# Self-attention's folded values as three fp32r passes over 128 tokens, with odd heads in swapped sequence order

## The reference, cut to what matters

```python
qkv = x @ w_qkv                      # 16 heads of 64, x is the layernormed residual
scores = einsum('bhid,bhjd->bhij', q, k) / sqrt(64)
attn = softmax(where(mask, scores, -inf), axis=-1)   # mask is causal for 64 tokens
out = einsum('bhij,bhjd->bhid', attn, v)
x = x + out.reshape(b, s, 1024) @ w_out
```

## Time and profile before

| | |
|---|---|
| median of 3 runs | 2475.48 us (2474.33 to 2478.04) |
| the profiled execution | 2475.1 us |
| its span, first to last instruction | 2473.1 us |
| PE busy | 2310.8 us, 93% of the span |
| DVE busy | 2117.5 us, 86% |
| mean granted TensorE clock | 0.974 |

### The profile page before, as it was taken

One profiled execution on the slowest core, in us unless ns is written; L12 is line 12 of the kernel. 1 busy time (PEld: TensorE's weight loads), 2 busy tenths in 40 slices (PEclk: granted clock), 3 DMA queues, 4 the chain that ended last, 5 costly groups with the idle time before them and its releaser, 6 DMA issues. The chain is left out here.

```text
span 2473.1 us, 57460 instructions
## 1 busy us (share of the span) xinstructions
PE 2310.8 (93%) x16359; PEld 1935.2 (78%) x16359; DVE 2117.5 (86%) x3384; ACT 1333.1 (54%) x2566; POOL 1528.0 (62%) x1117
## 2 busy tenths in 40 slices
PE   6988999999999999999999999999999998999842
PEld 3666888888888888888888888888888878776522
DVE  6779999998999999999999999999999995576657
ACT  4744555555555555555555555555555534355440
POOL 3424777777777777777777777777777750011155
PEclk8999999999999999999999999999999999999965
DMA  2432122222222222222222222222222226220000
GB/s 81 164 121 47 43 52 58 55 53 53 53 53 52 53 61 53 52 52 52 61 53 53 56 63 52 53 53 52 52 52 52 52 80 191 70 70 2 2 1 17
DMA packets 441099, 145.04 MB, mean 59 GB/s; under 512 B 365344, under 2 KB 423616, under 8 KB 440896
## 3 DMA queue, kind: packets, MB, share of 16 engines
q1 hardware_dynamic: 440880, 143.50, 23.4%
q10 hardware_dynamic: 144, 0.52, 0.1%
HBM read 109.17 MB, written 34.73 MB: 58 GB/s over the span
## 5 line engine op out<-in xcount | busy, mean ns | idle before, releaser
L451 POOL TENSOR_TENSOR probs<-arena,best_all 128x1024 f32 (+2 forms) x397 | 944.0, 2378 | 420.8 <-DVE best L817 398.9
L1061 PEld LDWEIGHTS u_ps<-rows,probs 128*128 128x128 f32 x6656 | 800.1, 191 | 54.7 <-issue 13.3
L1061 PE MATMUL u_ps<-rows,probs 128*128 (+1 forms) x6656 | 810.8, 275 | 9.1 <-ACT probs L648 5.0
L802 DVE SCALAR_TENSOR_TENSOR arena<-s_ps,mask,rrms 128x512 f32 (+2 forms) x832 | 604.0, 727 | 113.4 <-PE s_ps L938 111.7
L648 ACT ACTIVATE probs<-probs 128x1024 f32<-128x1024 f32 (+1 forms) x416 | 441.0, 1061 | 415.0 <-POOL probs L451 401.7
L778 DVE TENSOR_REDUCE ssq<-squares 128x16 f32<-128x1024 f32 (+1 forms) x416 | 501.2, 1205 | 34.7 <-ACT squares L606 34.7
L606 ACT ACTIVATE squares<-k_ps 128x512 f32<-128x512 f32 (+1 forms) x832 | 451.3, 591 | 50.1 <-DVE ssq L778 25.1
L817 DVE TENSOR_TENSOR best<-best,arena 128x1024 f32<-128x1024 f32 (+1 forms) x352 | 446.3, 1268 | 0.1
L936 PE MATMUL k_ps<-w_hi,cT_hi 128*128 128x512 f32 (+1 forms) x832 | 361.9, 435 | 12.4 <-ACT squares L606 12.3
L487 POOL TENSOR_TENSOR cT_lo<-cT,cT_hi 128x128 fp32r<-128x128 f32 (+1 forms) x416 | 296.9, 714 | 107.3 <-ACT cT_hi L600 107.3
L936 PE MATMUL s_ps<-q_hi,cT_hi 128*128 (+2 forms) x832 | 330.4, 397 | 2.1 <-DVE arena L802 1.8
(11 more groups left out here) (224 smaller groups left out, 2174.4 us busy)
## 6 DMA issues: line engine op xcount, KB each, us to landing
stage<-in_ctx SPq DMA_DIRECT2D x1536, 16.0 KB, 1.7
rows<-in_ctx SPq DMA_DIRECT2D x32, 768.0 KB
queries<-probs SPq DMA_DIRECT2D x16, 1024.0 KB, 4.0
q_plain<-queries SPq DMA_DIRECT2D x32, 512.0 KB, 3.3
best_all<-best_rows SPq DMA_DIRECT2D x31, 512.0 KB, 3.6
u_transposed<-uT_sb SPq DMA_DIRECT2D x124, 128.0 KB, 2.6
a_uT<-u_transposed SPq DMA_DIRECT2D x10, 1024.0 KB, 4.9
arena<-u_transposed SPq DMA_DIRECT2D x6, 1024.0 KB, 5.0
```

The costliest lines, as they stand in the source:

```text
L451: pool.tensor_tensor(probs[0:r, slot_of(c, PRING), :], scores_at(b, c), best_all[0:r, bass.ds((b % 2) * HL, HL)], ALU.subtract).then_inc(s ...
L802: dve.scalar_tensor_tensor(out=scores_at(p, c, h * HALF, HALF).rearrange("p (h l) -> p h l", l=L), in0=s_ps[h][0:r, :].rearrange("p (h l) ...
L1061: last = pe.matmul(u_ps[g // 3][:, at:at + UW], probs[0:r, s, g * P:(g + 1) * P], rows, start=(c == 0 and g % 3 == 0), stop=(c == NC - 1), ...
```

## The change

The folded values are computed in the same way as q and k: both operands are split into an fp32r high part and a low part, and each bank gets three fp32r matmuls of all 128 tokens by 512 columns. With 128 tokens as the stationary operand, the sequence b lands on PSUM partitions 64b to 64b+63. `mix` needs even and odd heads on different rows, so for the odd heads the tokens are taken in swapped order. To have the swapped order as one slice, each tile now takes 192 columns of yT_hi and yT_lo: its 128 tokens and its first 64 again. Which head of a pair a row group r serves is now `r ^ b` in `score` and `mix`; the probability tiles, the banks a_sc and a_ov and v2 are laid out by r instead of by odd.

- Gone: the tile yT and its copy on ACT (L1296, 128x128), the semaphore yT_ready.
- New on ACT: a copy of 128x64 for each tile, and in steps -9 to -6 one copy of 128x512 (wvo2_hi).
- New on DVE: a subtraction of 128x64 for each tile, and in steps -9 to -6 one subtraction of 128x512 (wvo2_lo), ahead of the quantizing.
- PE: `project_v` issues 12 fp32r matmuls of 128x128 by 128x512 instead of 8 fp32 ones of 128x64 by 128x512; `project_qk` reads its 512 tokens as four pieces of 128 with a step of 192; the order of array rows in `score` changes for b = 1.

```diff
@@ self_attention, PE
             def project_v(t, i):
-                pe.wait_ge(yT_ready, t + 1)
+                pe.wait_ge(yT_lo_ready, 2 * t + 2)
+                pe.wait_ge(wvo2_ready, 4)
...
-                    b, h = divmod(k, 2)
-                    at = t % 12 * P + b * L
-                    for odd in range(2):
-                        last = pe.matmul(four[k][odd * L:(odd + 1) * L, :], yT[:, at:at + L],
-                                         w["wvo2"][:, odd * HL + h * HALF:odd * HL + (h + 1) * HALF], start=True, stop=True)
-                    last.then_inc(v_ps, 1)
+                    tokens = window(t, k // 2)
+                    pe.matmul(four[k][:, :], yT_hi[:, tokens], wvo2_hi[:, half(k)], start=True, stop=False)
+                    pe.matmul(four[k][:, :], yT_lo[:, tokens], wvo2_hi[:, half(k)], start=False, stop=False)
+                    pe.matmul(four[k][:, :], yT_hi[:, tokens], wvo2_lo[:, half(k)], start=False, stop=True).then_inc(v_ps, 1)
@@ score
-                        for odd in range(2):
+                        for r in range(2):
+                            odd = r ^ b
                             rows = slice(odd * HD, (odd + 1) * HD)
-                            last = pe.matmul(sc[odd][b * L:(b + 1) * L, g * L:(g + 1) * L], q[rows, g, mine], k[rows, g, mine],
+                            last = pe.matmul(sc[r][b * L:(b + 1) * L, g * L:(g + 1) * L], q[rows, g, mine], k[rows, g, mine],
@@ mix
-                        for odd in range(2):
-                            rows = slice(odd * L, (odd + 1) * L)
+                        for r in range(2):
+                            rows = slice(r * L, (r + 1) * L)
...
-                            last = pe.matmul(ov[odd][b * L:(b + 1) * L, 0:D], w["pT"][rows, at:at + L],
-                                             w["v2"][t % 2][rows, b * HL + g * D:b * HL + (g + 1) * D],
+                            odd = r ^ b
+                            last = pe.matmul(ov[r][b * L:(b + 1) * L, 0:D], w["pT"][rows, at:at + L],
+                                             w["v2"][t % 2][rows, odd * HL + g * D:odd * HL + (g + 1) * D],
@@ ACT, step i
-                    act.activation(yT_hi[:, at:at + P], work[1][:, 0:P], ACT.Copy).then_inc(yT_hi_ready, 1)
...
-                    act.activation(yT[:, at:at + P], work[1][:, 0:P], ACT.Copy).then_inc(yT_ready, 1)
+                    act.activation(yT_hi[:, window(t)], work[1][:, 0:P], ACT.Copy).then_inc(yT_hi_ready, 1)
+                    act.activation(yT_hi[:, again(t)], work[1][:, 0:L], ACT.Copy).then_inc(yT_hi_ready, 1)
+                if -9 <= i < -5:
+                    part = half(i + 9)
+                    act.activation(wvo2_hi[:, part], w["wvo2"][:, part], ACT.Copy).then_inc(wvo2_hi_ready, 1)
@@ DVE, step i
-                    dve.wait_ge(yT_ready, t + 1)
...
-                    dve.tensor_tensor(yT_lo[:, at:at + P], work[1][:, 0:P], yT_hi[:, at:at + P], ALU.subtract).then_inc(yT_lo_ready, 1)
+                    dve.wait_ge(yT_hi_ready, 2 * t + 2)
+                    dve.tensor_tensor(yT_lo[:, window(t)], work[1][:, 0:P], yT_hi[:, window(t)], ALU.subtract).then_inc(yT_lo_ready, 1)
+                    dve.tensor_tensor(yT_lo[:, again(t)], work[1][:, 0:L], yT_hi[:, again(t)], ALU.subtract).then_inc(yT_lo_ready, 1)
...
+                if -9 <= i < -5:
+                    part = half(i + 9)
+                    dve.wait_ge(wvo2_hi_ready, i + 10)
+                    dve.tensor_tensor(wvo2_lo[:, part], w["wvo2"][:, part], wvo2_hi[:, part],
+                                      ALU.subtract).then_inc(wvo2_ready, 1)
```

More of the change, by code:

```diff
@@ L1154 @@
 QK_PARTS = 4
+WINDOW = P + L
 def upto(step, ahead, most=TILES):
@@ L1185, in self_attention @@
         wqk_lo = sb("a_wqk_lo", [P, 2 * HL], F32R)
-        yT_hi = sb("a_yT_hi", [P, 2 * HALF], F32R)
-        yT_lo = sb("a_yT_lo", [P, 2 * HALF], F32R)
-        yT = sb("a_yT", [P, 3 * HALF])
+        yT_hi = sb("a_yT_hi", [P, 2 * 4 * WINDOW], F32R)
+        yT_lo = sb("a_yT_lo", [P, 2 * 4 * WINDOW], F32R)
+        wvo2_hi = sb("a_wvo2_hi", [P, 2 * HL], F32R)
+        wvo2_lo = sb("a_wvo2_lo", [P, 2 * HL], F32R)
         uT = sb("a_uT", [P, 2, 2 * HL])
@@ L1210, in self_attention @@
         y_var, y_log, y_rough, y_ready, y_turned = (sem(f"a_{n}") for n in ("y_var", "y_log", "y_rough", "y_ready", "y_turned"))
-        yT_hi_ready, yT_ready, yT_lo_ready = sem("a_yT_hi_ready"), sem("a_yT_ready"), sem("a_yT_lo_ready")
+        yT_hi_ready, yT_lo_ready = sem("a_yT_hi_ready"), sem("a_yT_lo_ready")
+        wvo2_hi_ready, wvo2_ready = sem("a_wvo2_hi_ready"), sem("a_wvo2_ready")
         qk_ps, qk_saved, v_ps, v_saved = sem("a_qk_ps"), sem("a_qk_saved"), sem("a_v_ps"), sem("a_v_saved")
@@ L1227, in p_of, with window, again, group @@
             return w["p"] if t % 2 == 0 else p_odd
+        def window(t, swapped=0):
+            at = t % 8 * WINDOW + swapped * L
+            return slice(at, at + P)
+        def again(t):
+            at = t % 8 * WINDOW + P
+            return slice(at, at + L)
+        def group(part, j):
+            at = j % 2 * 4 * WINDOW
+            return part[:, at:at + 4 * WINDOW].rearrange("p (t n) -> p t n", n=WINDOW)[:, :, 0:P]
         def by_head(ap):
@@ L1334, in softmax_shift @@
             def softmax_shift(t):
-                p3 = p_of(t)[:, :].rearrange("p (h q j) -> p h q j", q=2, j=L)
+                p3 = p_of(t)[:, :].rearrange("p (h r j) -> p h r j", r=2, j=L)
                 if t >= 2:
@@ L1448, in turn_y @@
                 pe.wait_ge(qk_saved, parts_upto(i - 1))
-                pe.wait_ge(yT_lo_ready, t)
+                pe.wait_ge(yT_lo_ready, 2 * t)
                 pe.transpose(work[1][:, 0:P], y[:, t % 3 * D:(t % 3 + 1) * D], ident[:, :]).then_inc(y_turned, 1)
             def project_qk(j, r, i):
-                pe.wait_ge(yT_lo_ready, 4 * j + 4)
+                pe.wait_ge(yT_lo_ready, 2 * (4 * j + 4))
                 pe.wait_ge(w_ready, 1)
@@ L1461, in project_qk @@
                     if k == 3:
-                        pe.wait_ge(yT_lo_ready, upto(i, TURN_Y_AHEAD))
+                        pe.wait_ge(yT_lo_ready, 2 * upto(i, TURN_Y_AHEAD))
                     g = slice((4 * r + k) * P, (4 * r + k + 1) * P)
[L1464 to L1467, removed]
+                    pe.matmul(four[k][:, :], wqk_hi[:, g], group(yT_hi, j), start=True, stop=False)
+                    pe.matmul(four[k][:, :], wqk_hi[:, g], group(yT_lo, j), start=False, stop=False)
+                    pe.matmul(four[k][:, :], wqk_lo[:, g], group(yT_hi, j), start=False, stop=True).then_inc(qk_ps, 1)
             def project_v(t, i):
-                pe.wait_ge(yT_ready, t + 1)
+                pe.wait_ge(yT_lo_ready, 2 * t + 2)
+                pe.wait_ge(wvo2_ready, 4)
                 for k in range(4):
@@ L1487, in score @@
                 pe.wait_ge(qk_saved, 16 * (t // 4) + 16)
-                for odd in range(2):
-                    pe.wait_ge(masked, max(0, 2 * (t - 1) + odd + 1))
+                for r in range(2):
+                    pe.wait_ge(masked, max(0, 2 * (t - 1) + r + 1))
                 q, k = (w["qk"][j][:, n * 4 * HL:(n + 1) * 4 * HL].rearrange("p (g n) -> p g n", n=HALF) for n in range(2))
```

9 lines of the change are left out of this document (3 added, 6 removed).

## The result

The change makes the kernel faster, by a quarter of a percent: the median is 2468.55 us (2464.43 to 2473.08, 9 runs), that of the kernel before in the same rounds 2474.33 (2469.16 to 2478.04, 9 runs), a ratio of 0.9975 [0.9964, 0.9986]. The profiled execution took 2468.55 too, with a span of 2466.8. The forecast was 2470.0, its range 2467.6 to 2476.0. Of all executions behind this document one, in e7, was in a slow state and took 4671.11 us; its ratio leaves it out.

The account below looks back on a forecast made before the run. PE was taken to set the pace where folded values are computed, with ACT's last save 0.34 us ahead of it. Terms 1.64-1.44-1.20-1.32-2.58-0.64 = -5.54 took 2475.1 to 2469.6; with 0.4 for the median, 2470.0 us, range 2467.6 to 2476.0.

Parts of the forecast that it names:

- The folded values: PE from the folded values' start to the scores: 3.58 us becomes 2.84, saving PE 0.83 a tile.
- The start: Steps -9 to -5: DVE's new subtractions are on the path in steps -7 and -6, costing +1.64 us, bounds 1.1 and 2.1.
- The third 0.14: Part of the start's cost: the second yT_lo in step -5, ahead of PE's fourth qk bank, costs 0.14 us.
- Steps -4 to -1: Steps -2 and -1 gain 0.83 us each, less 0.08 and 0.14 for the longer yT_lo: -1.44.
- Steps 0 to 5: ACT's v saves hold the period at 14.06 us, PE idles 0.63; 0.20 gained per step, -1.20 in all.
- Step 6 and steps 7 to 10: Step 6 gains 1.32 us through an earlier mask and cheaper folded values; steps 7 to 10, with alternating periods, gain 2.58.
- The tail: Steps 11 on: only step 12, 9.27 us from `turn_p` to the mask, gains, 0.64; the others none.
- Rival 1: Score block doubles from 1.09 to 2.18 us as both row groups write each bank: 2481.3 us, 8%; small stretch 13%.
- Rival 2: Longer PE idle before `sum_heads` in step -5 brings half clock onto the path: cost 1.5 to 2.8 us, 12%.
- Rival 3: Nothing waits for ACT, so PE gains 0.83 us in all 13 steps from -2 to 10: 2465.9 us, 6%.
- Rival 4: The second yT_lo runs after POOL's pass, so steps 0 to 5 gain nothing: 2471.2 us, 7%.

Follow-up runs that it names:

- e7: Changed kernel without the values' middle pass (yT_lo times wvo2_hi), `turn_p` waiting only for the first two v banks: 2452.62 us, ratio 0.9924 to the kernel before.
- e10: Changed kernel with one plain fp32 matmul of 128 tokens per v bank, the tokens' low part left out: 2472.14 us, ratio 0.9996 to the kernel before.
- e8: Changed kernel with only DVE's wvo2_lo subtractions moved to steps -9, -8, -4 and -3, ACT's copies unmoved: 2465.35 us, ratio 0.9965 to the kernel before.
- e4: Changed kernel with DVE's wvo2_lo subtractions and ACT's wvo2_hi copies in steps -9, -8, -4 and -3: 2466.8 us, ratio 0.9979 to the kernel before.
- e1: Changed kernel with `turn_p` waiting only for the first two v banks to be saved: 2465.48 us, ratio 0.9969 to the kernel before.
- e6: Changed kernel without the middle pass of the folded values (yT_lo times wvo2_hi), wait of `turn_p` kept: 2461.54 us, ratio 0.996 to the kernel before.
- e2: Kernel before the change, with `turn_p` waiting only for the first two v banks to be saved: 2472.93 us, ratio 1.0006 to the kernel before.
- e11_after_again: Changed kernel timed again unaltered, as baseline of the third set: 2466.55 us, ratio 0.9974 to the kernel before.
- e3: Kernel before the change, folded values still plain fp32, with only the new row order in `score` and `mix`: 2472.2 us, ratio 1.0 to the kernel before.
- e5: Changed kernel with both the shorter `turn_p` wait of e1 and the later wvo2 split of e4: 2462.87 us, ratio 0.9964 to the kernel before.
- e9: Changed kernel with DVE's later subtractions of e8 and the shorter `turn_p` wait of e1: 2462.04 us, ratio 0.9955 to the kernel before.

## Why the prediction was right, point by point

- **The folded values.** Forecast 2.84, measured 2.81. e10 shows that the old block's price was that of plain fp32 and not of the pairs: 0.88 a bank is 3.8 passes of 0.229, so the saving is about one pass in four. The Trainium skill, "FP8 and Floating Point Precision", section "TensorE Precision Notes", gives true FP32 four passes through the array; the 3.8 of e10 agrees.
- **The start.** +1.64 was +1.30. Right in kind: each of the two steps grew, e8 takes the two subtractions away from there and gets 1.20 back. The pitch of wvo2_lo was 0.60, the second yT_lo 0.13:

```profile
2110.29 0.68 DVE L1403 TENSOR_TENSOR a_wvo_lo<-arena,a_wvo_hi 128x512 fp32r<-128x512 f32 x1
2110.89 0.54 DVE L1145 TENSOR_REDUCE a_ws<-ffn_w 128x12 f32<-128x384 f32 x1
...
2113.41 0.28 DVE L1384 TENSOR_TENSOR x_then_z<-a_work,x_then_z 128x128 f32<-128x128 f32 x1
2113.89 5.32 PE L1449 MATMUL a_work<-arena 128*64 128x128 f32 x64 [2.24 <-DVEq L1385]
...
2122.03 0.50 PE L1489 MATMUL a_work<-a_yT_hi,a_wqk_hi 128*128 128x512 f32 x1 [0.47 <-DVE a_yT_lo L1394]
...
2123.23 3.71 PE L1449 MATMUL a_work<-arena,a_uT 128*64 128x128 f32 x64 [0.24 <-ACT arena L1322]
```

  The last two rows in the kernel before, where the adds started at 2108.74 and, two steps on, 2119.82:

```profile
2122.14 0.51 PE L1465 MATMUL a_work<-a_yT_hi,a_wqk_hi 128*128 128x512 f32 x1 [0.96 <-DVE a_yT_lo L1375]
...
2123.48 3.71 PE L1425 MATMUL a_work<-arena,a_uT 128*64 128x128 f32 x64 [0.37 <-ACT arena L1303]
```

  From add to add, the two steps went from 11.08 to 12.43 (2107.19 to 2119.62), so by 1.35; 2 x (0.60 + 0.13) is 1.46. The mis-sized term is 3 x 0.14. In the two steps ACT's second copy is shorter than the one it replaces, so DVE waits about 0.06 less a step ahead of yT_lo (0.78 against 0.84), which I had counted in step -2 alone. The third 0.14, in step -5, is not on the path at all. The longer yT_lo does delay PE's fourth qk bank, to 2.41 after the add from 2.32. But the next `sum_heads`, with which the stretch ends, waits for ACT's qk saves, and it starts 3.61 after the add, where it was 3.66. 1.35 less 0.05 is the stretch's 1.30.
- **Steps -4 to -1.** -1.44 was -1.60. Steps -2 and -1 gave 0.78 and 0.72, so 1.50; the other 0.10 comes from steps -4 and -3, which I had at nothing. ACT's second copy is 0.05 shorter, and e4 shows that ACT ahead of its qk saves is on PE's path just there.
- **Steps 0 to 5.** Forecast 14.06 with PE idle 0.63, measured 14.02 to 14.07 with 0.56 to 0.64. e1 shows that the wait is for ACT's last saves, since without it PE comes round in 13.4; e6 shows that a still cheaper PE gains nothing; e2 that before the change the wait decided nothing in these steps. This is where the expected 0.83 a tile went: 0.22 a step arrived, 0.6 became a wait.
- **Step 6 and steps 7 to 10.** -1.32 and -2.58 were -1.33 and -2.64, with the periods alternating as said, 10.51, 10.12, 10.46 and 10.14. PE in the changed kernel at the end of step 6 and at the heads of steps 7 and 8:

```profile
2251.04 0.50 PE L1489 MATMUL a_work<-a_yT_hi,a_wqk_hi 128*128 128x512 f32 x1 [0.57 <-DVE a_yT_lo L1394]
...
2254.71 1.16 PE L1520 MATMUL a_sc<-arena 64*64 64x64 f32 x64
2255.80 1.09 PE L1433 MATMUL a_tp<-ident,a_p_odd 128*128 128x128 f32 x8
...
2266.31 1.06 PE L1433 MATMUL a_tp<-ident,arena 128*128 128x128 f32 x8 [0.32 <-ACT arena L1329]
```

  The wait for yT_lo fell from 1.07 to 0.57: 0.50 for the 0.49 forecast. In e1, with the last saves out of the way, the periods of steps 7 to 10 are 10.12 to 10.14 and the alternation is gone.
- **The tail.** -0.64 was -0.38. From `turn_p` of step 12 to the mask behind it 9.27 was to lose 0.64, and with it the period of step 13. It lost 0.36 (the mask starts at 2316.42, 8.91 after the first row below), because `mix` in that step ran longer, 3.34 against 2.60, and ended 4.75 after T instead of 4.47, although `turn_p` was shorter:

```profile
2307.51 1.15 PE L1433 MATMUL a_tp<-ident,arena 128*128 128x128 f32 x8 [3.06 <-ACT arena L1329]
...
2308.92 3.34 PE L1464 MATMUL a_ov<-arena 64*64 64x128 f32 x64 [0.26 <-ACT arena L1300]
```

  In e11_after_again, the same kernel, that `mix` took 1.98, and steps 11 to 14 took 36.84, so -0.83. But e10, with the old price of the folded values and also a `mix` of 1.98, took 36.93. With the granted clock at 1.00 in step 12, the mask starts 8.55 after T in e10 and 8.55 in e11, behind DVE's own work and with no wait for the scores; here are both, from T = 2310.85 and 2308.65:

```profile
2319.40 1.28 DVE L1361 SCALAR_TENSOR_TENSOR arena<-a_sc,a_seen 128x512 f32<-128x512 f32 x2
```

```profile
2317.20 1.28 DVE L1361 SCALAR_TENSOR_TENSOR arena<-a_sc,a_seen 128x512 f32<-128x512 f32 x2
```

  The 9.27 of the earlier trace rows had half clock in it (`turn_p` at 1.94, a granted clock of 0.50 there). So the term was right about PE's work and wrong about what it is worth: at full clock the change gains about 0.1 in the tail, and -0.38 and -0.64 are both a matter of where the clock falls.
- **Rival 1, slower scores,** falls by e3 and by the changed kernel's score block (2255.80-2254.71 = 1.09 above), with each bank written from both row groups, other rows for b = 0 than for b = 1. The Trainium skill, "TensorEngine Tiling (Array Packing)", section "Restrictions and Gotchas", says that different row tiles cannot access one PSUM bank at the same time. The prediction read a doubled block from it, and that did not come. Whether two of these tiles, which write different partitions of the bank, were in it in the same instant no run shows, so the sentence itself is neither borne out nor refuted here.
- **Rival 2, half clock on the path,** happened and cost nothing. The `sum_heads` of step -5 above took 5.32 instead of 3.71 after an idle of 2.24 (forecast 2.3). Its granted clock was 0.69 on average. It ran beside DVE's longer step: DVE's add behind it, at 2119.62, had no idle time before it, and PE's fourth qk bank behind it still waited 0.47 for yT_lo (2122.03 above). The next `sum_heads` had its full speed, 3.71, as said. In e4, e5, e8 and e9, where DVE's subtractions for wvo2_lo are gone from these steps, it takes 3.71 after an idle of 1.63. The start's cost is DVE's own, then, not the clock's.
- **Rival 3, nothing waits for ACT,** falls by e6 and is what e1 makes of the kernel.
- **Rival 4, the second yT_lo held by POOL,** falls by the rows of DVE and POOL above. What the Trainium skill, "SBUF — State Buffer", section "SBUF: two separate sides", says of operands, that a DVE operation with two SBUF inputs and a GpSimd one exclude each other, fits again: the two subtractions that read PSUM ran beside POOL in 0.29 and 0.22, the 128x1 one behind them was held for 1.63.

Some of the match is luck. The terms are off by 0.01 to 0.34 and in part cancel (-5.99 for -5.54), and the unpriced parts happened to come to only -0.4 in this pair of profiles. The 1.45 between 2470.0 and 2468.55 is for the most part the starting point: the forecast was counted from a median of 2475.48, and that of the same rounds was 2474.33. That about 6 us is the change's own is supported by the two later sets, in which the medians differ by 6.3 each (2472.11 and 2465.8, 2472.82 and 2466.55).

One thing stays open: e1's median did not show its 3.9, while e5's and e9's show the same edit.

## What to carry to other kernels

When the busiest engine gets cheaper, ask in each stage who is next and by how much: such margins, like the 0.34 us between ACT's last save and PE's arrival, priced 13 us of saved PE time at 5.5. Then look at what that new wait is really for: it covered four banks where two were needed, and cutting it to these, with two subtractions moved off the start, brought another 5.0 us in steps -8 to 10. And look at the clock of a row before pricing with it: the tail's 9.27 held a half-clock stretch, and its 0.64 with it. Work moved to an engine with idle time must be checked against what stands behind it in that engine's order: ACT was busy for 17.23 of the 37.30 us of steps -4 to -1, and a copy of 0.63 there still cost 0.5 a step.

## What was not expected of the hardware

- The array's two row groups write one bank, in different partitions, with no loss that shows: 1.09 for 64 records of 64x64 in either order.
- A pair of fp32 matmuls of 64 columns of the array each, side by side, costs nearly what one of 128 costs: 3.58 against 3.52 for the block.
- The stretches from step -8 to step 10 repeat to within 0.07, but the parts that do not change move by more than the edits are worth. The first `sum_heads` of self-attention started anywhere from 2082.46 (e9) to 2088.91 (e4), steps -10 and -9 took between 10.9 and 14.0 according to whether the `sum_heads` of step -9 took 3.71, 5.4 or 6.5, and from the first transpose of `ffn` to the end it was 122.5 to 124.2. Changes of 1 to 4 us in this kernel are read from stretches, not from one median.
